# The skip term of a state-memory layer: from a diagonal product on TensorE to a multiply and an add on GpSimd

## The reference, cut to what matters

```
...
content = Bm * x[..., :STATE]
cphi, sphi = (jnp.cos(phi), jnp.sin(phi))
memory_real = jnp.cumsum(content * cphi, axis=1)
memory_imag = jnp.cumsum(content * sphi, axis=1)
retrieved = Cm * (memory_real * cphi + memory_imag * sphi)
y = retrieved @ W_out + b_out + D * x
...
x = x + _L1_attn_ref(_layernorm(x, axis=-1), ...)
x = x + _L1_ffn_ref(_layernorm(x, axis=-1), ...)
```

## Time and profile before

| what | value |
|---|---|
| runs, us | 1604.21, 1598.77, 1598.38; median 1598.77 |
| the profiled execution, us | 1608.24, its span 1606.3 |
| busy in the span, us | PE 1293.9, PE weight loads 720.0, DVE 1022.1, ACT 800.9, POOL 543.6 |
| stage of the change | about 690 to 1062 us of the span |
| lead-in, 690 to 840 us: busy | PE 86.8, DVE 98.9, ACT 80.9, POOL 90.8 of 150; TensorE's clock 0.68 |
| 840 to 975 us: busy | PE 121.8, DVE 104.2, ACT 69.5, POOL 63.3 of 135; clock 1.00 |
| 975 to 1062 us: busy | PE 78.4, DVE 29.3, ACT 23.5, POOL 34.1 of 87; clock 0.94 |

### The profile page before, as it was taken

How to read it: one execution, slowest core, us unless ns; L and a number is a source line. 1 busy time by engine, 2 the same in 40 slices (tenths; PEclk the granted TensorE clock), 3 DMA queues, 4 the chain that set the end, 5 groups by cost and what they waited for, 6 DMA issues and landing times. The chain is left out here.

```text
span 1606.3 us, 21908 instructions
## 1 busy us (share of the span) xinstructions
PE 1293.9 (81%) x6692; PEld 720.0 (45%) x6692; DVE 1022.1 (64%) x2759; ACT 800.9 (50%) x1604; POOL 543.6 (34%) x717
## 2 busy tenths in 40 slices
PE   5899999999994238925689989956999995899497
PEld 1233333333322228912355556543666664677232
DVE  7778888888834655626878784323566654566355
ACT  2467777776773004526655544212554543566244
POOL 3342344233110024367355452410221113242066
PEclk7799999999997559965699999975999997899799
DMA  5111111111106202210223323411113130000001
GB/s 150 53 51 40 42 51 44 42 48 47 35 1 176 47 13 59 54 35 20 44 53 71 54 54 70 91 35 56 60 57 109 61 106 20 1 1 1 14 21 33
DMA packets 80774, 81.15 MB, mean 51 GB/s; under 512 B 19899, under 2 KB 64139, under 8 KB 80659
## 3 DMA queue, kind: packets, MB, share of 16 engines
q1 hardware_dynamic: 77327, 74.06, 17.5%
q0 software_dynamic: 2304, 4.72, 1.3%
q10 hardware_dynamic: 1028, 0.98, 0.2%
HBM read 64.32 MB, written 13.92 MB: 49 GB/s over the span
## 5 line engine op out<-in xcount | busy, mean ns | idle before, releaser
L960 DVE TENSOR_REDUCE a_nm<-a_aps 128x1 f32<-128x512 f32 x512 | 333.6, 687 | 74.6 <-PE a_aps L725 74.5
L924 ACT ACTIVATE a_prob<-a_sps 128x512 f32<-128x512 f32 x512 | 271.1, 597 | 114.3 <-PE a_sps L737 113.6
L725 PE MATMUL a_aps<-a_K,a_Q 96*128 96x512 bf16 x512 | 194.9, 401 | 12.3 <-DMA a_K<-k_parts 12.1
L737 PE MATMUL a_sps<-a_Q,a_K 99*128 99x512 bf16 x512 | 156.1, 384 | 1.2 <-ACT a_prob L924 1.2
L1429 POOL TENSOR_TENSOR p_h<-p_sl,p_t 128x512 f32<-128x512 f32 x72 | 105.6, 1485 | 143.1 <-ACT p_sl L1569 55.2
L746 PE MATMUL a_ops<-a_prob,a_Vg 128*32 128x512 f32 x1024 | 137.5, 611 | 0.0
L725 PEld LDWEIGHTS a_aps<-a_K,a_Q 96*128 96x128 bf16 x512 | 50.2, 98 | 139.8 <-DVE a_nm L960 90.0
L1569 ACT ACTIVATE p_sl<-p_up_a 128x512 f32<-128x512 f32 x72 | 42.9, 597 | 112.8 <-PE p_up_b L1459 112.8
L1955 POOL TENSOR_TENSOR c_h<-c_h,c_G 128x512 f32<-128x512 f32 x24 | 31.8, 1328 | 180.7 <-ACT c_h L2141 180.7
L434 POOL CAST a_ms<-a_mr 16x128 bf16<-16x128 f32 x32 | 9.0, 282 | 242.4 <-ACT a_mr L882 242.4
L1459 PE MATMUL p_up_b<-x_normT,p1w_w 128*128 128x512 f32 x144 | 76.4, 613 | 8.1 <-DVE p_t L1677 8.0
(11 more groups left out here) (526 smaller groups left out, 2676.8 us busy)
## 6 DMA issues: line engine op xcount, KB each, us to landing
p_G<-gates_by_expert SPq DMA_DIRECT2D x32, 512.0 KB
c_G<-choice_rows SPq DMA_DIRECT2D x32, 512.0 KB, 6.4
a_Q<-q_parts SPq DMA_DIRECT2D x192, 32.0 KB
a_K<-k_parts SPq DMA_DIRECT2D x31, 96.0 KB
q_parts<-a_partsq SPq DMA_DIRECT2D x7, 384.0 KB, 2.8
k_parts<-a_partsk SPq DMA_DIRECT2D x7, 384.0 KB, 2.8
token_outputs<-m0e_y SPq DMA_DIRECT2D x40, 64.0 KB, 1.5
m0w_w<-in_L_ffn_W SPq DMA_DIRECT2D x1, 2048.0 KB, 8.7
```

The source lines that it names most:

```text
L725: nc.tensor.matmul(aps[n % 3][:, :], Q[0:MAX, head, q * P:(q + 1) * P], K[0:MAX, head, :], start=True, stop=True).then_inc(a_ready, 1)
L737: nc.tensor.matmul(sps[(NS * u + k) % 3][:, :], K[0:KB, head, k % TC * P:(k % TC + 1) * P], Q[0:KB, head, :], start=True, stop=True).then_ ...
L924: nc.scalar.activation(prob[u % 2][:, k // TC, k % TC, :], sps[n % 3][:, :], ACT.Exp).then_inc(p_done, 1)
L960: nc.vector.tensor_reduce(nm[u % 2][:, s:s + 1], aps[n % 3][:, :], AX.X, ALU.max, negate=True).then_inc(a_used, 1)
```

## The change

The column Dc becomes a table `Db` with the vector D on every partition, loaded in Dc's place in the list. The matrix Dg, its instruction on GpSimd, the semaphore diag and TensorE's wait for it go. `outer` keeps only the products with Wo. `first_normal` gets two more instructions on GpSimd behind the bias: the normalised chunk times Db into a new tile `past`, and x plus past; VectorE's add_memory waits for the second of them (`past_added`) where it waited for bias_added.

```
-            (self.Dc, col(a("D"))), (self.gw, f("gate_w")), (self.b1, col(a("b_dt1"))),
+            (self.Db, row(a("D")).to_broadcast([P, D])), (self.gw, f("gate_w")), (self.b1, col(a("b_dt1"))),
...
                 nc.gpsimd.tensor_tensor(xt, xt, over_tiles(bo[:, :], TC), ALU.add).then_inc(bias_added, 1)
+                wait(pool, past_added, c)
+                nc.gpsimd.tensor_tensor(past[:, :, :], xn1[c % 2][:, :, :], over_tiles(Db[:, :], TC), ALU.mult).then_inc(past_done, 1)
+                pool.wait_ge(past_done, c + 1)
+                pool.wait_ge(bias_added, c + 1)
+                nc.gpsimd.tensor_tensor(xt, xt, past[:, :, :], ALU.add).then_inc(past_added, 1)
...
-            nc.gpsimd.tensor_scalar(Dg[:, :], net.ident[:, :], Dc[:, :], None, ALU.mult).then_inc(diag, 1)
...
-                    nc.tensor.matmul(ops[:, tok], r[c % 2][:, tok], Wo[:, :], start=True, stop=False)
-                    last = nc.tensor.matmul(ops[:, tok], net.xT[:, c * S + q * P:c * S + (q + 1) * P], Dg[:, :],
-                                            start=False, stop=True)
+                    last = nc.tensor.matmul(ops[:, tok], r[c % 2][:, tok], Wo[:, :], start=True, stop=True)
...
-            pe.wait_ge(diag, 1)
...
-                v.wait_ge(bias_added, c + 1)
+                v.wait_ge(past_added, c + 1)
```

More of the change, by code:

```diff
@@ L1304, in __init__ @@
         self.W1, self.W2 = p.sb("W1", [P, T1]), p.sb("W2", [T1, P])
-        self.bB, self.bC, self.b2, self.om0, self.Dc = (p.sb(n, [P, 1]) for n in ("bB", "bC", "b2", "om0", "Dc"))
-        self.b1, self.bo, self.gw = p.sb("b1", [T1, 1]), p.sb("bo", [P, D]), p.sb("gw", [P, E])
+        self.bB, self.bC, self.b2, self.om0 = (p.sb(n, [P, 1]) for n in ("bB", "bC", "b2", "om0"))
+        self.b1, self.bo, self.Db, self.gw = p.sb("b1", [T1, 1]), p.sb("bo", [P, D]), p.sb("Db", [P, D]), p.sb("gw", [P, E])
         self.w1, self.w3, self.w2 = (p.sb(n, [P, NP + 1, P]) for n in ("w1", "w3", "w2"))
@@ L1339, in memory_and_swiglu @@
         WB, WC, Wo, W1, W2, gw, w1, w3, w2 = mw.WB, mw.WC, mw.Wo, mw.W1, mw.W2, mw.gw, mw.w1, mw.w3, mw.w2
-        bB, bC, b2, om0, Dc, b1, bo = mw.bB, mw.bC, mw.b2, mw.om0, mw.Dc, mw.b1, mw.bo
-        Dg, turns, half_pi, one = p.sb("Dg", [P, P]), p.sb("turns", [P, 1]), p.sb("half_pi", [P, 1]), p.sb("one", [P, S])
+        bB, bC, b2, om0, Db, b1, bo = mw.bB, mw.bC, mw.b2, mw.om0, mw.Db, mw.b1, mw.bo
+        past, turns, half_pi, one = p.sb("past", [P, TC, D]), p.sb("turns", [P, 1]), p.sb("half_pi", [P, 1]), p.sb("one", [P, S])
         back, bst0 = [p.sb(f"back{c}", [P, TC, D]) for c in range(B)], p.sb("bst0", [P, TC, 6])
@@ L1360, in memory_and_swiglu @@
         yps, ops, bps, cps = p.ps("yps", [P, TC, D]), p.ps("ops"), p.ps("bps"), p.ps("cps")
-        consts, padded, diag = (p.sem(n) for n in ("consts", "padded", "diag"))
+        consts, padded, past_done, past_added = (p.sem(n) for n in ("consts", "padded", "past_done", "past_added"))
         back_loaded, x_added, bst0_done, stat0_done = ([p.sem(f"back_loaded{c}") for c in range(B)], p.sem("x_added"),
```

## The result

The changed kernel took 1605.01 us (median of its runs, 1599.39 to 1611.85). The kernel before, run beside it, took 1600.13 (1595.31 to 1607.66). The ratio is 1.0025 with a 95% interval of [1.0014, 1.0036]: 4.0 us slower, between 2.2 and 5.8. A second comparison, on a chip on which both need about 1610 us, gave 1.0003 [0.9985, 1.0021], 0.5 us slower. Weighed by their intervals the two make about 3 us, and both lie within half a per cent of no change. The forecast was 1599.2 us, 0.45 above before. The measured median, 1605.01, is 0.3 us above the upper end of the forecast's range (1604.7), but the range was built on 1598.77 us for the kernel before, which ran 1.4 us longer beside the change. The ratio applied to 1598.77 gives 1602.8: inside the range, and above the forecast's own stretch (1597 to 1601.5).

A forecast was written before the change was run, and what follows sets the result against it. VectorE was taken as nearly full in the lead-in, TensorE in steps 0 to 7 but largely hidden by other chains. Gains 4.1 - 0.25 against 4.3 lost: 0.45 us slower, 1599.2 us; range 1594 to 1604.7.

The forecast's parts named there:

- the forecast's own stretch: Whole time: the range of 1597 to 1601.5 us given to the main forecast, with chance 0.50.
- The gains in the lead-in: Lead-in: Dg's removal at the head gains 0.62, shorter outer of chunks 0, 1, 2 gains 1.35, 0.43, 0.87; 0.25 lost.
- The holds: Lead-in steps -3 to -1: GpSimd's new two-input instructions hold VectorE in chunks 3, 4, 5 by 1.0, 2.1, 1.2; cost 4.3.
- the hold that the bias add no longer makes: Chunk 4's step: bias add no longer meets VectorE's L1699, but VectorE then waits for logits; 0.5 us taken off.
- GpSimd's queue at no cost: Lead-in: GpSimd's delay is absorbed by its waits for the factors; cost 0, at worst up to 2 us.
- Chunks 3, 4 and 5 hidden behind ScalarE's copy: Steps 0 to 2: logits wait for ScalarE's copy, not outer, so removing these products gains 0.
- The forecast's last sign of being wrong: Memory stage: the forecast is wrong if the stage outside the lead-in changes by more than 1 us.
- Chunk 7's 0.85: Step 4: shorter outer lets logits, gates and their transfer start earlier; gain 0.85 us.
- TensorE's clock moves: Rival, lead-in: less TensorE work makes the clock rise later, costing 2 to 3 us, 1602 us; chance 0.05.

The follow-up runs named there:

- e1: Kernel before without the skip term: TensorE's diagonal products and Dg gone, nothing new on GpSimd; ratio 0.9999 to the kernel before.
- f2: Kernel before with the skip term of chunks 0, 1 and 2 left out, TensorE's product kept for 3 to 7; 3.9 us shorter than before.
- g1: The changed kernel run again, unaltered, in another comparison with the kernel before; ratio 1.0003, 0.5 us over before.
- f4: Changed kernel with GpSimd's multiply and add replaced by two equally long memsets in chunks 0 to 5, skip term left out; -0.2 us against before.
- g4: The kernel before, unchanged, profiled a second time; 267.2 us behind the lead-in against 264.3 in its first profile.
- e2: Kernel before with all TensorE products kept, plus GpSimd's multiply and add in all chunks into a scratch tile; ratio 1.0015 to before.
- e3: Kernel before with the skip term moved to GpSimd for chunks 3, 4 and 5 only; +2.7 us against before.
- f1: Kernel before with the skip term moved to GpSimd for chunks 0, 1 and 2 only, diagonal made late; ratio 0.9961, 6.3 us shorter than before.
- g2: Changed kernel plus an unused identity product on TensorE in chunks 3 to 7 in place of the diagonal one; ratio 1.0001 to before.
- g3: Repeat of the kernel with GpSimd doing the skip term for chunks 0, 1 and 2 only; ratio 0.9971, 4.7 us shorter than before.
- e4: Kernel before with the skip term moved to GpSimd for chunks 0, 1, 2, 6 and 7, diagonal made late; 2.6 us shorter than before.
- f3: Kernel before with the skip term of chunks 3 to 7 left out, TensorE's product kept for 0 to 2; 1.4 us longer than before.

## Why the forecast came out as it did

The lead-in came out as forecast, to within 0.6 us. What the forecast missed lies behind it, where it had put all removed products but chunk 7's at nothing.

**The gains in the lead-in** (0.62 at the head, 1.35, 0.43, 0.87, less 0.25: 3.0) were real and a little small. e1 has 3.43, f2 3.10, both with the head's 0.62 in them.

**The holds** (4.3) were right in kind and size. After's lead-in is 106.25 - 102.09 = 4.2 us longer than e1's. By the adds of chunks 0, 1 and 2 the 4.2 came as 1.4, 2.1 and 0.7; the forecast had 1.0, 2.1 and 1.2. VectorE's net hold of 4.7 is near this by chance: 1.4 of it cost nothing, and 1.15 us of waiting for the logits stand in for the hold that the bias add no longer makes, where the forecast had allowed 0.5. The tensor_scalar instructions with one SBUF input were held as much as the two-input ones. Net of gains, the head's included, the lead-in should have been 1.3 us longer; it was 0.73, and 1.24 in g1.

**GpSimd's queue at no cost** stands. turn_first did wait 31.4 us for GpSimd's `p_xn` where it waited 26.3, and add_back 26.2 us for its transfers where it waited 20.7. By the forecast's own words that would have refuted it. But these waits replace others: in after memory of chunk 0 starts as early as in e1 (48.50 and 48.54 us), and in f4, with a queue about as late, one hold explains all but some 0.3 us of the lead-in.

**Chunks 3, 4 and 5 hidden behind ScalarE's copy** stands as a statement on the path (1.12 for 0.23 at the logits). What it missed is that "hidden" did not mean free. The hidden products filled TensorE's gap, and at four of 18 such gaps the clock fell. The forecast's last sign of being wrong, a change of more than 1 us outside the lead-in, showed: 3.7 us in the stage behind it, 2.2 against the mean of before's two profiles.

**Chunk 7's 0.85** did not come as time: the logits' reader is 0.9 us later instead of 0.85 earlier. The path was read rightly; the clock on it was not what the forecast took it to be. From the second transposes to that reader it takes 3.25 us with the product at full clock (before, g4, e2) and 4.84 to 4.88 with the product where the clock fell (e3, f1, f2, g2, g3). Without the product it takes 4.16 in after and 4.13 in e1, which had the whole stretch at the lower clock, 0.7 us less than with it. No run shows it without the product at full clock. Nor is the product in chunk 7 what kept the clock up. The wait ahead of the transposes is 2.42 to 2.46 us in all 14 profiles, and the clock fell behind it in all eleven profiles of kernels that lack the diagonal product of any chunk, g2 with its filler among them, and in none of the three of kernels that have all. Why a kernel that lacks only chunks 0 to 2 falls there, some 170 us later, stays open.

The falls there differ in length: between 957 and 977 us the six kernels without a product in chunk 7 lost 3.4, 1.7, 3.4, 3.4, 1.7 and 3.4 us of clock (after, g1, e1, e4, f3, f4), on average 2.8; of the eight profiles with one, before, g4 and e2 lost none, and e3, f1, f2, g2 and g3 1.7 each, on average 1.1.

**The rival "TensorE's clock moves"** had 0.05 and was put in the lead-in. It belonged behind it. To size it, take each ratio times 1610.6 us and subtract what is accounted for: the lead-in from the table, which holds the 0.62 of the head, and 0.85 where chunk 7 lost its product.

```
                             measured   lead-in, chunk 7       rest
no product in chunks 3 to 7
  after                        +4.0     +0.73 -0.85            +4.1
  g1                           +0.5     +1.24 -0.85            +0.1
  e1                           -0.2     -3.43 -0.85            +4.1
  f3                           +1.4     +0.15 -0.85            +2.1
  f4                           -0.2     +0.19 -0.85            +0.5
a product in some of them
  e3 (6, 7)                    +2.7     +1.06  0               +1.6
  e4 (3, 4, 5)                 -2.6     -2.59 -0.85            +0.8
a product in all of them
  e2                           +2.4     +2.76  0               -0.4
  f1                           -6.3     -2.36  0               -3.9
  g3                           -4.7     -2.23  0               -2.5
  f2                           -3.9     -3.10  0               -0.8
  g2 (filler)                  +0.2     +0.85  0               -0.7
```
Each rest is uncertain by some 2 to 3 us. The first group's mean is +2.2, the last one's -1.6: 3.8 us apart. The profiles' clock lost is 15.4 us on average in the first group and 10.8 in the last with both profiles of before added, 4.6 apart, and the mean clock 0.8787 against 0.8812, which is 4 us of 1610. The profiles' own lengths behind the lead-in, 268.5 us on average against 266.3, are 2.2 apart, 3.1 with the 0.85. So the products that the forecast took for free were worth about 3 to 4 us of clock.

That the clock falls without them and returns with a filler is shown; that this is the whole of the lost time rests on the groups, which were put together after the fact. Of the direct pairs, e1 and f2 (3.7 us, give or take 2.8) agree with it, and g1 and g2 (1.2, give or take 2.4) resolve nothing. Open remain, too, whether part of after's +4.0 in the first comparison was chance (g1 says +0.5), why f1 and g3 are 2.5 to 4 us better than the account, and whether it is the products' work or the changed timing that keeps the clock up; no kernel moved the gaps without adding or taking work.

Forecast and result by terms, in us: lead-in with the head +1.3 (was +0.7 to +1.2); behind it -0.85, all of it chunk 7's (was about +2, the difference to the 3 of the two comparisons). So some 3 us, put at nothing under "hidden", are missing behind the lead-in, and that the result still lies near the forecast owes something to luck.

## What to carry to other kernels

Work of an engine that is hidden behind another's chain is not free to take away where the engine is TensorE: look at what gap it leaves, and at the granted clock on both sides, before counting zero. Move such work chunk by chunk rather than as a whole. Here the three chunks of the lead-in, where TensorE ended last, gave 5.4 us (2.3 of them seen in the lead-in); moving the other five as well gave that back. A GpSimd instruction beside VectorE's tensor_scalar or two-input instructions on SBUF can hold VectorE up to its own end, and for several in a row up to the end of the last. The hold costs time only where VectorE isn't about to wait anyway: 3.5 us of holds cost 1.1 in e3. So place such instructions beside VectorE's work on PSUM or its waits.

## What the runs showed of the hardware

- A GpSimd memset held a VectorE tensor_scalar for 3.74 us instead of 0.44, through the bias add and two memsets in a row. In chunk 4 of after, where semaphore waits stand between GpSimd's instructions, VectorE's held instruction ended 0.28 us after the multiply, at 765.04, and not after the add.
- The hold works both ways: GpSimd's 128x512 multiply took 1.26 us at least, 1.49 at the median and 2.23 at most in after, the long ones beside VectorE's SBUF instructions.
- An idle time of 0.93 us ahead of a few short products was followed by a fall of TensorE's clock at 4 of 18 places; without the idle time at 0 of 24.
- The same wait of 2.42 us ahead of the same transposes was followed by a fall in 11 of 14 profiles.
- Added TensorE work that nobody uses (20 products of 128x128, 40 matmul instructions) raised the program's mean granted clock from 0.8783 to 0.8814, and cost no time that could be measured.
